# Routing stage of a two-layer kernel: the key tiles of a chunk are added on VectorE ahead of one product with ones, and the one-hot products stand behind the second key tile

## What is computed

```python
xn = _layernorm(x)                                   # x: sum of layer 0
# linear attention: keys and values
k = gelu(xn @ Wk.T + bk) + 0.21
v = xn @ Wv.T + bv
k_r = _rope(k)
z = 1.0 / (einsum('bhnd,bhd->bhn', qh, kh.mean(axis=2)) + 1e-06)   # mean over the tokens
kv = einsum('bhnd,bhne->bhde', krh * scale, vh * scale)
# routing
scores = softmax(xf @ gate_w.T)
_, idx = top_k(scores + gate_b, 6)
order = argsort(idx.reshape(-1))                     # position of a token in its expert
z_shared = silu(xf @ ws1.T) * (xf @ ws3.T) @ ws2.T   # shared expert
```

## Time and profile before

| | us |
|---|---|
| median of 3 runs | 5882.93 (5879.49 to 5885.64) |
| the profiled execution, its own time | 5885.59 |
| span of the profiled execution (first to last instruction) | 5883.5 |
| TensorE busy | 5145.9 (87%) |
| VectorE busy | 4283.5 (73%) |
| ScalarE busy | 2960.2 (50%) |
| GpSimd busy | 2998.5 (51%) |
| mean granted clock of TensorE | 0.942 |
| `route`: first and last instruction of the chunk loop and its tail on VectorE | about 4808 to 5360 |

### The profile page before, as it was taken

One profiled execution on the slowest core, in us unless ns is written; L12 is line 12 of the kernel. 1 busy time (PEld: TensorE's weight loads), 2 busy tenths in 40 slices (PEclk: granted clock), 3 DMA queues, 4 the chain that ended last, 5 costly groups with the idle time before them and its releaser, 6 DMA issues. The chain is left out here.

```text
span 5883.5 us, 80028 instructions
## 1 busy us (share of the span) xinstructions
PE 5145.9 (87%) x26286; PEld 3061.8 (52%) x26286; DVE 4283.5 (73%) x8723; ACT 2960.2 (50%) x6282; POOL 2998.5 (51%) x1603
## 2 busy tenths in 40 slices
PE   6788778777775899998999899999989989998877
PEld 2222222222231677776555566666655555556745
DVE  3999999999999798886333677777743337784249
ACT  4776776776774677774111455555521114342233
POOL 4999899899888455553111444444411100003724
PEclk9888998899886899999999999999999999999988
DMA  5565665556563222222111111111121134344565
GB/s 135 144 150 140 144 153 143 136 147 149 132 144 85 92 87 87 87 87 67 54 54 47 49 34 36 33 33 33 32 58 54 54 122 141 129 134 126 150 200 185
DMA packets 503856, 598.15 MB, mean 102 GB/s; under 512 B 59782, under 2 KB 381332, under 8 KB 499348
## 3 DMA queue, kind: packets, MB, share of 16 engines
q1 hardware_dynamic: 484308, 582.36, 36.0%
q10 hardware_dynamic: 6848, 8.67, 0.5%
q0 software_dynamic: 12288, 2.00, 0.3%
HBM read 429.38 MB, written 180.37 MB: 104 GB/s over the span
## 5 line engine op out<-in xcount | busy, mean ns | idle before, releaser
L654 POOL TENSOR_TENSOR db<-durep,brep 128x2048 f32<-128x2048 f32 x256 | 1161.0, 4535 | 188.8 <-DVE p_h L561 178.2
L513 ACT ACTIVATE p_h<-dlrep,am 128x512 f32<-128x512 f32 x1024 | 704.5, 691 | 196.4 <-DVE hh L572 171.3
L561 DVE TENSOR_TENSOR_SCAN p_h<-p_h,hlast,db 128x512 f32<-128x512 f32 x576 | 720.2, 1283 | 0.0
L1213 POOL TENSOR_TENSOR rn<-n,mhalf 128x16 f32<-128x16 f32 x128 | 374.8, 2929 | 630.3 <-DVE n L1160 630.2
L349 PE MATMUL p_acc<-hh,fold 128*32 128x512 f32 x2048 | 316.5, 694 | 343.0 <-DVE hh L572 341.7
L572 DVE TENSOR_TENSOR hh<-p_h,crep 128x512 f32<-128x512 f32 x768 | 519.9, 677 | 0.0
L1538 POOL TENSOR_TENSOR grstd<-grstd,mhalf 128x4 f32<-128x4 f32 x32 | 32.6, 1018 | 788.2 <-DVE grstd L1465 788.2
L1217 POOL TENSOR_TENSOR rot_cos<-rot_cos,rot_sin 128x1024 f32<-128x1024 f32 x128 | 301.9, 2359 | 220.9 <-DVE rot_sin L1150 220.9
L946 PE MATMUL p_o<-probT,v 128*64 128x128 f32 x4096 | 407.4, 280 | 7.3 <-DVE probT L1133 3.9
L1030 ACT ACTIVATE probT<-p_t 128x512 f32<-128x512 f32 x256 | 152.7, 597 | 480.1 <-PE p_t L933 480.1
L946 PEld LDWEIGHTS p_o<-probT,v 128*64 128x64 f32 x4096 | 345.3, 137 | 91.0 <-issue 70.7
(11 more groups left out here) (277 smaller groups left out, 11926.8 us busy)
## 6 DMA issues: line engine op xcount, KB each, us to landing
dlrep<-delta_rows SPq DMA_DIRECT2D x256, 256.0 KB
durep<-drive_rows SPq DMA_DIRECT2D x256, 256.0 KB
ew<-in_L_ffn_w SPq DMA_DIRECT2D x192, 176.0 KB
first_queries_keys<-qs SPq DMA_DIRECT2D x128, 256.0 KB, 2.1
qk<-first_queries_keys SPq DMA_DIRECT2D x64, 512.0 KB, 3.8
brep<-bc_rows SPq DMA_DIRECT2D x64, 256.0 KB
crep<-bc_rows SPq DMA_DIRECT2D x64, 256.0 KB
delta_rows<-dl SPq DMA_DIRECT2D x64, 256.0 KB
```

What stands on the lines that cost most here:

```text
L513: act.activation(p_h[:, (i % BANKS) * CH:(i % BANKS + 1) * CH], dlrep[use % 2][:, j], ACT.Exp, scale=am[:, q, j, g:g + 1]).then_inc(s_ex, 1)
L561: dve.tensor_tensor_scan(out=state, data0=bank, data1=db[s % 2][:, j], initial=0.0 if first else hlast[:, i % TILES:i % TILES + 1], op0=AL ...
L654: pool.tensor_tensor(out=db[s % 2][:], in0=durep[use % 2][:], in1=brep[c % 2][:, g:g + 1, :].to_broadcast([P, 4, CH]), op=ALU.mult).then_i ...
L1213: pool.tensor_tensor(out=rn[f % 2][:], in0=n2[f % 2][:], in1=mhalf[:], op=ALU.pow).then_inc(s_rn, 1)
```

## The change

- VectorE's `rotate(c)` begins with `k2`, the sum of key tiles 0 and 1 with key tiles 2 and 3 (512 elements per partition), and has, between the two halves of `kt` and the sum that makes `kr`, the further `k1`, the sum of the two halves of `k2` (256 elements).
- TensorE's `key_sums` multiplies ones with `k1`, one product in place of four, and waits for `s_k1`.
- On TensorE `keys(c, 1)` moves ahead of `invert(c - 1)`.
- On VectorE `collect(c - 1)` moves from between `keys(c, 0)` and `keys(c, 1)` to behind `normalise(c + 1)`.

```diff
@@ route
     kr, kt = (sb(n, [P, CT, D]) for n in ("kr", "kt"))
+    k2, k1 = sb("k2", [P, 2, D]), sb("k1", [P, D])
...
+    s_k2, s_k1 = sem("r_k2"), sem("r_k1")
...
@@ tensor: key_sums
                 pe.wait_ge(s_kg, c + 1)
-                for j in range(CT):
-                    pe.matmul(p_ks, ones[:], kg(c)[:, j], start=(u == 0 and j == 0), stop=False, skip_group_check=True)
+                pe.wait_ge(s_k1, c + 1)
+                pe.matmul(p_ks, ones[:], k1[:], start=(u == 0), stop=False, skip_group_check=True)
                 pe.wait_ge(s_kr, c + 1)
...
@@ tensor: the loop
                 keys(c, 0)
+                keys(c, 1)
                 if c > 0:
                     invert(c - 1)
-                keys(c, 1)
-                if c > 0:
                     key_sums(c - 1)
...
@@ vector: rotate
                     dve.wait_ge(s_kr, c)
+                dve.scalar_tensor_tensor(out=k2[:], in0=kg(c)[:, 0:2], scalar=0.0, in1=kg(c)[:, 2:4], op0=ALU.add,
+                                         op1=ALU.add).then_inc(s_k2, 1)
                 dve.scalar_tensor_tensor(out=kr[:], in0=kg(c), scalar=KB, in1=cs[:, u, :, 0], op0=ALU.add, op1=ALU.mult)
                 for e in range(2):
...
                 ins.then_inc(s_krs, 1)
+                dve.wait_ge(s_k2, c + 1)
+                dve.scalar_tensor_tensor(out=k1[:], in0=k2[:, 0], scalar=0.0, in1=k2[:, 1], op0=ALU.add,
+                                         op1=ALU.add).then_inc(s_k1, 1)
                 dve.wait_ge(s_krs, c + 1)
...
@@ vector: the loop
                 keys(c, 0)
-                if c > 0:
-                    collect(c - 1)
                 keys(c, 1)
                 if c + 1 < NC:
                     normalise(c + 1)
+                if c > 0:
+                    collect(c - 1)
```

## The result

| | us |
|---|---|
| median after | 5913.36 (5910.35 to 5915.78, 5 runs) |
| median before, on the same chips | 5882.86 (5873.78 to 5885.64, 5 runs) |
| ratio | 1.0054, 95% interval 1.0042 to 1.0065 |
| forecast | 5928, range 5893 to 5941 |
| span of the profiled execution | 5912.5 (before 5883.5) |

The kernel is 30.5 us slower: the forecast side, with a size of 30.5 where 45 was forecast.

A forecast was written before the change was run, and what follows sets the result against it. It took VectorE's chain up to the first `sh`, not TensorE, to bound `route`. VectorE's additions 12.2, falling clock 31 and tail 2 gave 45 us on 5885.6, 5930.6, less 2.7 for the median: 5928, range 5893 to 5941.

The forecast's parts named there:

- The bound: In `route`, `shared(c, 1)` waits for VectorE's first `sh`; 23 of 33 us per chunk go by VectorE, 10 by TensorE.
- VectorE's additions, 0.81 us per chunk, 12.2 us: In `rotate`, `k2` costs 0.60 and `k1` 0.21 us, paid in full ahead of `lsub`: 12.2 us in all.
- The idle time of 3.7 us: TensorE sits idle 3.7 us in one piece before `shared(c, 1)` in each of chunks 1 to 14.
- The clock, "14 x 2.2 = 31 us": TensorE's clock falls in the idle time before `shared(c, 1)` in all 14 chunks: 31 us (22 to 38).
- The price of a fall: Time lost per clock fall from `shared(c, 1)` on: 2.2 us, the middle of 1.6 and 2.7.
- the 29 stretches of the earlier trace: In `mamba`, 29 groups of L349 behind 3.5 to 4.2 us of TensorE idle time, all but one slowed.
- The tail, 0.8 + 2: After the last chunk, VectorE's additions paid in full, and TensorE's products slow after 5 us idle: 2 us (0 to 3.5).
- Nothing for `collect`: Moving `collect` behind `normalise` on VectorE costs nothing, as its reader `positions` comes only after 3.7 us of `shared(c, 1)`.
- The rival that the clock holds: TensorE's clock stays up in `route`, leaving only VectorE's 12.2 us: 5895; chance 10%.
- the third rival: In `route`, the clock falls more cheaply or the two additions overlap better: half of each term, about 5903; chance 4%.

The follow-up runs named there:

- e1: Changed kernel plus three unused filler products of 512 columns behind `key_sums`, so TensorE idles less before `shared(c, 1)`: 5894.29 us, ratio to kernel before 1.0019.
- e10: Changed kernel with early first `sh`, one-column table loads on ScalarE, `collect` directly behind `choose`, `normalise` behind `keys(c, 2)`: 5840.03 us, 0.9928 of the kernel before.
- e2: Changed kernel without VectorE's two additions; one product of ones with the first key tile alone: 5916.53 us, ratio to kernel before 1.0055.
- e3: Kernel before with only the two moves (`keys(c, 1)` and `collect`), four products, no additions: 5895.30 us, ratio 1.0022.
- e6: Changed kernel with the first `sg` before the exponential and the first `sh` right behind `lsub`: 5899.08 us, ratio to kernel before 1.0023.
- e4: Kernel before with only the two additions and the one product, in the old order: 5894.66 us, ratio 1.0021.
- e8: e5 with the additions and the one product, but the old order (`invert` ahead of `keys(c, 1)`): 5900.6 us, ratio to kernel before 1.0026.
- e5: Kernel before with the first `sg` before the exponential and the first `sh` right behind `lsub`: 5887.66 us, ratio 1.0003.
- e9: Kernel before with e5's edit, one-column table loads on ScalarE, `collect` directly behind `choose`, `normalise` behind `keys(c, 2)`: 5870.51 us, ratio 0.9981.
- e12: Kernel before with only a one-column Exp ahead of ScalarE's wait for `lsub`: 5869.37 us, ratio 0.9978.

## Why the prediction was right, and what it mis-sized

- **The bound.** Right. The wait of `shared(c, 1)` for VectorE's `sh` decides (e1, e10): savings on TensorE ahead of it are worth nothing, and taking the wait away makes them worth 30 us.
- **VectorE's additions, 0.81 us per chunk, 12.2 us.** Right: 0.81 by the rows after, 33.93 against 33.14 us per chunk in e1, and 11.8 us in e1's median, its tail included. In e1's trace chunks 1 to 14 take 11.0 us more than before and the whole stage 15.1, since the last chunk is longer too and e1 fills no idle time of the tail; the 3 us between that and the median are of the size by which the other stages scatter.
- **The idle time of 3.7 us.** Right: 3.59.
- **The clock, "14 x 2.2 = 31 us".** This is the step that was mis-sized. The price of a fall was right in the mean, 2.2 us, and in part by luck: single falls cost 1.4 to 1.7 or 2.6 to 3.1 us, on both sides of the range of 1.6 to 2.7, and the 2.2 was its middle. The count was not right: 10 of 14. I took it from the 29 stretches of the earlier trace rows, all followed by a fall, though they are up to 0.6 us longer and TensorE's work around them holds further idle times (in the trace of before 1.54 and 1.81 us ahead of the groups of L349 at 1122.73 and 1135.73). e2, with the same 3.59 us and 14 of 14, shows that the length of one idle time does not fix the count. 10 x 2.2 in the forecast's sum gives 36 us for the stage, against 35.6 measured. Why the clock held in 4 of the 14 stays open.
- **The tail, 0.8 + 2.** Right: 2.7 us.
- **Nothing for `collect`.** Right for this kernel (in e3 a chunk without a fall has the old distance), for the reason given (TensorE is late); wrong as a property of the move (e6).
- **The rival that the clock holds** was excluded in the changed kernel; e1 produces it by force, and its 5895 was 5894.
- **A slip.** For the third rival, half of each term is 22.6 us, which gives 5905 and not 5903. Nothing hangs on it.
- **Open.** The stage grew by 35.6 us in one execution and the medians by 30.5. So of the 14.5 us between the forecast 45 and the measured 30.5, 9 are the count of falls in the trace and 5 are not explained by the stage. The untouched stages together took 5324 to 5335 us in the 14 profiled executions. The unchanged kernel scatters alike, and that with TensorE's clock: of 27 executions beside e1, those with a mean granted clock of 0.944 took 5875.6 and 5878.3 us, those with 0.941 took 5886.7 to 5888.4. The changed kernel had 0.937 in the profiled execution and 0.938 to 0.940 in the other four; that would allow for fewer falls there, but 0.001 is about 12 us at half clock, anywhere in the kernel, and so it can't be decided.

## What to carry to other kernels

Before moving or saving work on the busiest engine, find what its next wait waits for: TensorE was 93% busy here, and still VectorE's chain set the pace. Idle time on TensorE that is longer and in one piece can cost more than the work that was saved (e3: one of 2.29 us in place of 1.69 and 0.59), so look at the longest idle stretch after the change, not at the sum. And time a change again after the bound has moved: this one went from 30 us slower to 30 us faster.

## What was not expected of the hardware

- The same idle time of 3.59 us, with dense work around it, goes with a fall of the clock in 10 of 14 chunks (changed kernel) or 14 of 14 (e2). One of 2.29 us goes with a fall in 8 of 14 (e3), one of 2.25 us in 14 of 14 (e6), one of 2.50 us in 12 of 14 (e4) and 14 of 14 (e8). Idle times of 1.69 us never did (14 chunks before, and the same in e5, e9 and e12).
- The table loads ahead of the exponential and of the SiLU start only when the wait in front of the function has passed (1.28 us in e5, idle until then for 8.58 us). A one-column activation ahead of the wait takes the load off the chain (e12). This is not so for every function: ahead of the GELU, in the kernel before, the load starts 4.5 us before the function, and the wait comes behind it. In the code one `wait_ge` stands in front of the GELU and two in front of the other two functions; whether that decides it was not tried.

```profile
5063.10 1.28 ACT L1845 ACT_TABLE_LOAD   x1 [3.83 <-DVE lsub L1944]
5064.40 0.42 ACT L1845 ACTIVATE lex<-lsub 128x256 f32<-128x256 f32 x1
...
5082.79 1.28 ACT L1839 ACT_TABLE_LOAD   x1
5087.33 1.06 ACT L1839 ACTIVATE rks<-rks 128x1024 f32<-128x1024 f32 x1 [3.25 <-DVE rks L1912]
```
